# Attention rows transposed and scaled by one product with a diagonal matrix of inverse row sums

## What is computed

```python
energy = jnp.einsum('bnc,bcm->bnm', F_Fc, G_Fs)        # 1024 x 1024 per image
attention = jax.nn.softmax(energy, axis=-1)
H_Fs = conv1x1(content_feat, h_w, h_b).reshape(B, C, HW)
out = jnp.einsum('bcn,bmn->bcm', H_Fs, attention).reshape(B, C, H, W)
out = conv1x1(out, o_w, o_b)
return out + content_feat
```

## Time and profile before

| | before |
|---|---|
| median of three runs | 802.56 us |
| profiled execution, its own time | 800.25 us |
| its span, first to last instruction | 798.5 us |
| mean granted TensorE clock | 0.949 |
| PE busy | 686.6 us (86%) |
| DVE busy | 591.0 us (74%) |
| ACT busy | 498.0 us (62%) |
| POOL busy | 536.1 us (67%) |

### The profile page before, as it was taken

How to read it: one execution, slowest core, us unless ns; L and a number is a source line. 1 busy time by engine, 2 the same in 40 slices (tenths; PEclk the granted TensorE clock), 3 DMA queues, 4 the chain that set the end, 5 groups by cost and what they waited for, 6 DMA issues and landing times.

```text
span 798.5 us, 9550 instructions
## 1 busy us (share of the span) xinstructions
PE 686.6 (86%) x2952; PEld 470.9 (59%) x2952; DVE 591.0 (74%) x790; ACT 498.0 (62%) x715; POOL 536.1 (67%) x248
## 2 busy tenths in 40 slices
PE   4999979799889889899879879899979775798987
PEld 3844568476666458575665457565765453566743
DVE  6999299989767887989778887989778893334400
ACT  3754548975488758975498758875498754223730
POOL 3389869797788598797778698797778677000000
PEclk9999999999799899999799989999799987899999
DMA  5000020000000220000000220000000020000000
GB/s 202 1 1 0 0 106 1 2 1 0 1 1 1 80 80 0 0 0 0 0 0 0 79 80 0 0 0 0 0 0 0 26 79 0 1 1 0 1 26 27
DMA packets 4802, 15.95 MB, mean 20 GB/s; under 512 B 672, under 2 KB 928, under 8 KB 3744
## 3 DMA queue, kind: packets, MB, share of 16 engines
q1 hardware_dynamic: 4768, 15.56, 5.2%
HBM read 11.37 MB, written 4.19 MB: 19 GB/s over the span
## 4 chain that ended last, share of the span: by engine, by line
PE 52%; DVE 15%; ACT 14%; issue 12%; POOL 5%; DMA 1%; ACTq 0%; DVEq 0%; POOLq 0%; SPq 0%
PE ps L571 9%; PE ps L497 7%; PE ps L547 6%; DVE ps L965 5%; ACT prod L776 4%; PE ps L586 4%; PE ps L450 3%; PE ps L454 3%; PE ps L451 3%; PE ps L625 3%; PE ps L507 3%; PE ps L520 2%; POOL rows L1195 2%; POOL conv L1195 2%; PE ps L562 2%
## 5 line engine op out<-in xcount | busy, mean ns | idle before, releaser
L1195 POOL TENSOR_TENSOR conv<-conv,prod 128x930 f32<-128x930 f32 (+4 forms) x192 | 428.4, 2265 | 104.9 <-ACT prod L776 101.1
L965 DVE SCALAR_TENSOR_TENSOR ps<-raw,dw_sb,ps 128x960 f32<-128x960 f32 (+4 forms) x290 | 348.5, 1202 | 12.7 <-issue 4.4
L776 ACT ACTIVATE prod<-raw,dw_sb 128x930 f32<-128x930 f32 (+4 forms) x228 | 248.7, 1108 | 84.6 <-POOL conv L1195 74.0
L571 PE MATMUL ps<-kv,oc 128*128 128x512 f32 x256 | 113.0, 600 | 2.7 <-ACT kv L906 2.7
L1195 POOL TENSOR_TENSOR rows<-rows,prod 128x930 f32<-128x930 f32 (+4 forms) x36 | 81.8, 2273 | 13.5 <-ACT prod L776 10.8
L571 PEld LDWEIGHTS ps<-kv,oc 128*128 128x128 f32 x256 | 48.9, 192 | 62.5 <-issue 58.2
L1120 DVE TENSOR_REDUCE small<-ps 128x1 f32<-128x1024 f32 x32 | 39.2, 1224 | 47.2 <-PE ps L547 47.2
L562 PE MATMUL ps<-mask_sb,rows 128*128 128x128 f32 x256 | 40.0, 302 | 29.3 <-ACT kv L906 20.4
L520 PE MATMUL ps<-sd,rows 128*128 128x144 f32 x256 | 46.0, 307 | 16.7 <-DVE kv L1027 12.9
L625 PE MATMUL ps<-oc,proj_sb 128*128 128x512 f32 x128 | 56.0, 595 | 1.2 <-ACT oc L802 0.7
L562 PEld LDWEIGHTS ps<-mask_sb,rows 128*128 128x128 f32 x256 | 30.8, 152 | 42.6 <-ACT kv L906 23.7
(11 more groups left out here) (107 smaller groups left out, 1074.0 us busy)
## 6 DMA issues: line engine op xcount, KB each, us to landing
rows<-x_dram SPq DMA_DIRECT2D x4, 1024.0 KB, 4.9
x<-x_dram SPq DMA_DIRECT2D x4, 1024.0 KB, 4.8
out_dram<-x SPq DMA_DIRECT2D x8, 512.0 KB, 3.1
conv<-wqkv_dram SPq DMA_DIRECT2D x1, 768.0 KB, 4.5
conv<-fg_dram SPq DMA_DIRECT2D x1, 512.0 KB, 5.5
proj_sb<-proj_dram SPq DMA_DIRECT2D x1, 512.0 KB, 7.3
pw_sb<-pw_dram SPq DMA_DIRECT2D x1, 384.0 KB, 6.5
conv<-hw_dram SPq DMA_DIRECT2D x1, 256.0 KB, 5.7
```

What stands on the lines that cost most here:

```text
L571: mm = pe.matmul(ps[:, 4 + c, :], ht[:, j, c * P:(c + 1) * P], pt[:, j, :], start=(j == 0), stop=(j == NB - 1))
L776: act.activation(dst, view, ACT.Copy, scale=weight(t, i)).then_inc(prod_ready, 1)
L965: return dve.scalar_tensor_tensor(dst, view, w, before, ALU.mult, ALU.add)
L1195: pool.tensor_tensor(total, total, product, ALU.add).then_inc(conv_pool, 1)
```

## The change

ACT no longer scales the rows. DVE, right after the reciprocal, makes a 128 x 128 diagonal matrix of the inverse row sums from the identity, in one of three buffers, and TensorE multiplies each unscaled 128 x 128 piece of `rows`, held as the stationary operand, by this matrix instead of transposing it. The product is the transposed and scaled piece. The semaphores of `normalise` go, and T(i) waits for the diagonal.

```diff
-ROWS_ACT = (1, 1, 1, 1, 1, 1, 1, 1)
...
+        diag = sb("diag", [P, 3, P])
...
             def p_transposes(b, i):
 
-                pe.wait_ge(*rows_count(b, i))
+                pe.wait_ge(diag_ready, 8 * b + i + 1)
...
-                        mm = pe.transpose(ps[:, 4 + u, j * P:(j + 1) * P], rows[:, i % ROW_BUFS, key:key + P], ident)
+                        mm = pe.matmul(ps[:, 4 + u, j * P:(j + 1) * P], rows[:, i % ROW_BUFS, key:key + P],
+                                       diag[:, i % 3, :], start=True, stop=True)
                     mm.then_inc(t_full, 1)
...
-                def normalise(i):
-                    act.wait_ge(exp_done, 8 * b + i + 1)
-                    act.wait_ge(rcp_ready, 8 * b + i + 1)
-                    row = rows[:, i % ROW_BUFS, :]
-                    act.mul(row, row, row_rcp[:, i:i + 1]).then_inc(rows_act, 1)
...
-                    if 1 <= i <= NB and ROWS_ACT[i - 1]:
-                        normalise(i - 1)
...
                         dve.reciprocal(row_rcp[:, i - 1:i], row_sum[:, i - 1:i]).then_inc(rcp_ready, 1)
-                        if not ROWS_ACT[i - 1]:
-                            dve.wait_ge(rcp_ready, 8 * b + i)
-                            row = rows[:, (i - 1) % ROW_BUFS, :]
-                            dve.tensor_scalar(row, row, row_rcp[:, i - 1:i], None, ALU.mult).then_inc(rows_dve, 1)
+                        dve.wait_ge(rcp_ready, 8 * b + i)
+
+                        if i >= 4:
+                            dve.wait_ge(t_full, 16 * b + 2 * (i - 4) + 2)
+                        dve.tensor_scalar(diag[:, (i - 1) % 3, :], ident, row_rcp[:, i - 1:i], None,
+                                          ALU.mult).then_inc(diag_ready, 1)
                         taps(TAPS_ATT[i])
```

More of the change, by code:

```diff
@@ L273, in conv_seq_kernel @@
         rcp_ready = sem("rcp_ready")
-        rows_act = sem("rows_act")
-        rows_dve = sem("rows_dve")
+        diag_ready = sem("diag_ready")
         t_full = sem("t_full")
@@ L363, in tap_view @@
             return raw[:, t, o:o + SIDE * ROW].rearrange("p (y x) -> p y x", x=ROW)[:, :, 0:SIDE]
-        def rows_count(b, i):
-            mine = [k for k in range(NB) if ROWS_ACT[k] == ROWS_ACT[i]]
-            return (rows_act if ROWS_ACT[i] else rows_dve), len(mine) * b + mine.index(i) + 1
         def images(kv0, q0):
```

## The result

The changed kernel takes 809.33 us, the median of five runs (807.35 to 811.31), against 802.17 for the kernel before in runs beside it: ratio 1.0097, 95% interval 1.0071 to 1.0123. It is slower, by about 1%, where +1.1 us was forecast; the median lies 0.3 us above the range. The profiled execution took 811.31 us, its span 809.5, 11.0 more than before. It is the slowest of the five, with the lowest mean granted clock (0.951; the others have 0.953 to 0.960), so what the trace shows is 2 us more than the median.

A forecast was written before the change was run, and what follows sets the result against it. ACT was taken to set the pace of batches 0 to 2. Batches 0 to 3 gave -1.1, +0.05, +0.8 and +1.4, +1.1 us on the profiled 800.25, 803.7 on the median; range 796 to 809.

The forecast's parts named there:

- faster rival: DVE's diagonals in batches 0 to 2 do not wait for POOL's adds: together -7.3 us, 795.3; chance 0.25.
- likeliest case: The laid-out sum over the four batches: +1.1 us on the profiled execution, 803.7 on the median; chance 0.55.
- steps 1, 2: Batch 1, start of T(0) to last maximum: diag(0) waits for an add, PE waits 0.8 before T(1); stage gains 0.85 us.
- step 3: Last maximum to T(4): diag(6) waits 1.5 us for POOL's add, the final begins 14.4 after the maximum, T(4) 0.75 late.
- step 4: T(4) to the first product at the stage's end, at full clock: 8.65 us, against 9.38 before.
- Step 2: Batch 1, T(0) to last maximum: four T and five E, 21.4 us, plus 0.8 of waiting before T(1).
- slower rival: DVE sets the loop's pace, diagonals of turns 2 to 5 waiting 1.1 us each: 2.1 a batch, 810.0; chance 0.16.
- the three waits: Waits of diag(6) for POOL's add, in batches 0 to 2: 1.5 us each, possibly gone or 0.7 longer.

The follow-up runs named there:

- e8_accum: The changed kernel with DVE's diagonals made in the form that also writes out a sum, which is not used: 794.65 us, ratio 0.9922 to the kernel before.
- e7_diag6_late: The changed kernel with diag(6) made behind the nine taps and final(0, 0) instead of ahead of them: 799.99 us, ratio 0.9985 to the kernel before.
- e10_pause8: e8_accum with eight DVE operations into unused buffers added ahead of final(0, 0) in batches 0 to 2: 804.20 us, ratio 1.0037 to the kernel before.
- e1_odd: The changed kernel with each diagonal written 129 columns wide instead of 128, the last column unused: 809.69 us, ratio 1.0108 to the kernel before.
- e9_pause4: e8_accum with four DVE operations into unused buffers added ahead of final(0, 0) in batches 0 to 2: 799.05 us, ratio 0.9979 to the kernel before.
- e6_act_diag_b3: e5_act_diag with the last batch as in the kernel before, ACT's scaling and transposes: 799.22 us, ratio 0.9978 to the kernel before.
- e5_act_diag: The changed kernel with the diagonals made by ACT, where it scaled the rows before, and none by DVE: 799.15 us, ratio 0.9981 to the kernel before.

## Why the prediction was wrong

**What it had right.** T as 16 passes (1.95 to 2.05 us measured, 1.85 forecast), ACT off the path, the start of the next batch as the measure, and that a DVE diagonal waits for a POOL add. Batch 3 came out at +1.33 against +1.4, with all its diagonals at 0.28 to 0.29 us. The faster rival, diagonals that do not wait, was put at 795.3; e8_accum, which takes the waits away, gave 794.65. Only the likeliest case was laid out wrongly, in three steps, the same way each time. The lengths and differences below, for batches 0, 1 and 2, are from the profiled execution:

| step | forecast | measured | missed |
|---|---|---|---|
| first to last maximum, against before (steps 1, 2) | -1.9, -0.85, -0.85 | -1.3, +0.36, -0.19 | 2.5 |
| last maximum to `final` (step 3) | 14.4 each | 15.33, 14.64, 15.32 | 2.1 |
| `final` to product (step 4) | 9.4 each | 11.59, 9.52, 11.57 | 4.5 |
| batch 3 and start of the span, against before | +1.4; 0 | +1.33; +0.7 | 0.6 |

The last column adds to 9.7; forecast and measurement of the profiled execution are 9.9 apart. The medians (803.7 and 809.33) are 5.6 apart, so the table holds more than the usual miss.

**Step 2, the loop.** I let only diag(0) wait and argued that the others fall just behind an add, since ACT's products start from the same maximum and so keep their phase. That holds only while POOL idles between adds, as the 2.62 us before the add in the earlier trace rows do. In the loop after the change POOL runs eight adds without a break, each starting when the one before ends, and a diagonal meets them at any point. Turns of 4.4 to 4.8 us against 4.5 for two adds let the meeting point drift from turn to turn, until one diagonal in each batch has just missed its chance and waits a whole add (2.33, 2.45 and 2.33 us). This is the slower rival's wait, but neither its size nor its path. Its price was four waits of 1.1 us, 2.1 us a batch; they came as one of 2.05 to 2.17 (2.33 and 2.45 less 0.28) and fractions, and the loop missed by 0.6 to 1.2 us a batch. And the rival had PE wait in each turn, while PE reached V(0) about as early as laid out and only DVE came late. That the total came near the rival's 810 is partly chance, as steps 3 and 4 had the larger share.

**Step 3, diag(6).** The right wait at the right place, mis-sized: 1.5 us forecast, 2.0 in batches 0 and 2, 1.3 in batch 1. This follows from step 2. I had the add that it meets start 1.1 us after the last maximum, with 2.8 us between the last two maxima; as DVE was behind, these were 1.92 us apart in batches 0 and 2 (2.61 in batch 1) and the add started at 1.99 (1.30). So in batches 0 and 2 the diagonal met it at its start, and not 0.5 in. A further 0.48 us of idle time ahead of the diagonal I had not reckoned with; e8_accum, whose diagonals do not wait for POOL, does not show it there, and what it is stays open.

**Step 4, the clock.** The largest miss of the profiled execution. I wrote that the gaps close with the longer T, so I took the full clock. They do close in the loop; T(4), though, waits for a DVE that steps 2 and 3 had just made late. I had computed that DVE ends last there and did not ask what this does to the engine that waits: my own numbers have V(0) end 1.6 us before T(4) starts. PE stands for 3.33 us, and the clock falls in batches 0 and 2, 2.1 us each, where I had put a fall at 0.8. e7_diag6_late (a wait of 1.03 us, no fall) and e10_pause8 (a pause put in, falls in all three) show the link; batch 1 of the changed kernel and two batches of e1_odd, 2.86 to 2.89 us without a fall, show that it is not a matter of length alone. How many falls the other four executions had is not on record; their higher mean clocks fit with fewer.

**The range** let the three waits be 0.7 us longer, and the falls stay as before. It did not let them come together, though the second follows from the first, and it had no late DVE in the loop beside them. Its upper end of 809 was half the way to the slower rival; that the median lies only 0.3 us above it is luck.

## What to carry to other kernels

Before work is moved from ACT to DVE, see what POOL does at that time: a tensor_scalar from SBUF to SBUF beside POOL's adds costs its 0.28 us and, at worst, a whole add; the form that also writes out a sum costs 0.35 us (plus 0.08) and waits for none of them. Where an operation of one engine waits for another engine's, a mean wait is not the price: look for the place in the order where one wait stands ahead of a long queue, and then ask what the waiting PE does to its clock. A saving on the engine that sets the pace is worth only the distance to the next one, and with three engines close together that distance is best read by changing one part at a time.

## What the runs showed of the hardware

- DVE's diagonal waits for the rest of POOL's add: it takes 0.28 us alone and up to 2.45 beside adds of 2.24, with 128 or 129 columns. With an accumulator output it takes 0.35 us everywhere.
- Successive DVE operations with an accumulator output start every 0.27 us, though each is recorded with 0.34 and 0.08.
- A wait of PE of 2.35 us brought the granted clock down behind it in three stages of three (e10_pause8), one of 3.33 in two of two (the change); one of 2.86 to 2.89 did so in one of four (the change, e1_odd), and those of 1.03 to 1.28 in none of six (e7_diag6_late, e9_pause4).
- The same short transposes met the lower clock at different places: in e6_act_diag_b3 V(1) behind them takes 15.69 us, in the kernel before it takes 14.00 and the two transposes ahead of it take 3.69. With fp32 products in their place (e5_act_diag, the change) the granted clock stayed at 1.00 there. Whether the kind of instruction or PE's idle time does it was not separated.
